# Experts' second layer in products of 512 columns, their outputs turned behind the loop, and POOL copying the gather's indices

## The reference

```python
h = (x_flat @ W_gat).reshape(M, HEADS, NUM_EXPERTS)
a_src = (h * att_src).sum(-1)
a_dst = (h * att_dst).sum(-1)
e = jax.nn.leaky_relu(a_src[src] + a_dst[dst], negative_slope=0.2)
e_max = jax.ops.segment_max(e, dst, num_segments=M)
ee = jnp.exp(e - e_max[dst])
denom = jax.ops.segment_sum(ee, dst, num_segments=M)
alpha = ee / (denom[dst] + 1e-16)
msg = h[src] * alpha[:, :, None]
agg = jax.ops.segment_sum(msg, dst, num_segments=M).reshape(M, HEADS * NUM_EXPERTS) + b_gat
scores = _layernorm(agg, ln_gamma, ln_beta).reshape(M, HEADS, NUM_EXPERTS).mean(1)
topk_s, topk_i = jax.lax.top_k(scores, TOP_K)
w = jax.nn.softmax(topk_s, axis=-1)
for ei in range(NUM_EXPERTS):
    g = jnp.where(topk_i == ei, w, 0.0).sum(-1)
    hh = jax.nn.gelu(x @ W1[ei] + b1[ei], approximate=False)
    out = out + g[..., None] * (hh @ W2[ei] + b2[ei])
```

## Time and profile before

| | |
|---|---|
| median of 3 runs | 1071.52 us (1070.34 to 1073.87) |
| the profiled execution: its own time | 1072.75 us |
| its span | 1071.0 us |
| busy in the span | PE 793.4 (74%), DVE 668.0 (62%), PEld 519.7 (49%), ACT 355.3 (33%), POOL 180.1 (17%) |
| granted TensorE clock, mean | 0.869 of full speed |

### The profile page before, as it was taken

How to read it: one execution, slowest core, us unless ns; L and a number is a source line. 1 busy time by engine, 2 the same in 40 slices (tenths; PEclk the granted TensorE clock), 3 DMA queues, 4 the chain that set the end, 5 groups by cost and what they waited for, 6 DMA issues and landing times.

```text
span 1071.0 us, 15105 instructions
## 1 busy us (share of the span) xinstructions
PE 793.4 (74%) x4837; PEld 519.7 (49%) x4837; DVE 668.0 (62%) x1393; ACT 355.3 (33%) x552; POOL 180.1 (17%) x179
## 2 busy tenths in 40 slices
PE   4369920017999989989988788799759877662688
PEld 1212220016887878878853233444327555442477
DVE  3599778755656656646648777595664434435764
ACT  3421130004544544545542333430022443333451
POOL 5180010000000000000022000100001366773021
PEclk9589965557999999999999899999977988886599
DMA  8000000001000000000000000000012200010001
GB/s 310 0 1 1 1 0 0 2 39 42 2 1 0 0 0 0 0 0 0 0 0 1 0 0 0 2 1 0 2 42 16 8 7 7 7 6 4 3 21 59
DMA packets 15645, 15.63 MB, mean 15 GB/s; under 512 B 9664, under 2 KB 13376, under 8 KB 15216
## 3 DMA queue, kind: packets, MB, share of 16 engines
q1 hardware_dynamic: 12544, 14.00, 4.3%
q0 software_dynamic: 3056, 1.08, 1.7%
HBM read 10.42 MB, written 4.65 MB: 14 GB/s over the span
## 4 chain that ended last, share of the span: by engine, by line
PE 19%; DVE 16%; issue 12%; POOL 3%; DMA 2%; DVEq 2%; ACT 2%; POOLq 0%; PEldq 0%; PEld 0%; SPq 0%; ACTq 0%
PE banks L1557 17%; DVE kept L1229 2%; POOL rows_g L592 2%; DMA rows_g<-table_d,g_idx 2%; DVE wide_buf L1189 1%; DVE wide_buf L1195 1%; PE banks L1838 1%; DVE tie L1193 1%; DVE kept L1292 1%; DVE kept L1386 1%; DVE T L867 1%; DVE round_k L1291 1%; PE banks L1590 1%; DVE shared L1384 1%; ACT wide_buf L776 1%
## 5 line engine op out<-in xcount | busy, mean ns | idle before, releaser
L1138 DVE TENSOR_TENSOR wide_buf<-banks,small 128x1024 f32<-128x1024 f32 x72 | 88.2, 1225 | 117.9 <-ACT small L726 117.9
L1557 PE MATMUL banks<-wide_buf 128*128 128x256 f32 (+1 forms) x720 | 144.6, 349 | 0.0
L1557 PEld LDWEIGHTS banks<-wide_buf 128*128 128x128 f32 x720 | 122.3, 194 | 12.6
L1557 PEld LDWEIGHTS banks<-XP 128*128 128x128 bf16 (+1 forms) x1552 | 101.8, 132 | 47.2 <-DVE XP L992 27.6
L1557 PE MATMUL banks<-XP 128*128 128x32 bf16 (+1 forms) x1552 | 102.4, 213 | 29.5 <-DVE XP L992 27.4
L592 POOL DMA_INDIRECT rows_g<-table_d,g_idx x88 | 95.5, 1085 | 132.2 <-issue 100.4
L1557 PE MATMUL banks<-taps_w,small 128*128 128x128 f32 x618 | 92.2, 296 | 21.0 <-issue 21.0
L1557 PE MATMUL banks<-T,XP 128*128 (+1 forms) x128 | 73.7, 701 | 38.2 <-ACT XP L789 33.3
L1557 PEld LDWEIGHTS banks<-taps_w,small 128*128 128x128 f32 x618 | 85.6, 203 | 31.7 <-issue 22.0
L724 ACT ACTIVATE small<-banks,neg_x 128x512 f32<-128x512 f32 x72 | 49.6, 690 | 150.1 <-PE banks L1557 124.2
L1557 PE MATMUL banks<-shared,sel 128*128 x216 | 60.2, 385 | 32.8 <-DVEq L1131 26.0
(11 more groups left out here) (330 smaller groups left out, 1190.9 us busy)
## 6 DMA issues: line engine op xcount, KB each, us to landing
wide_buf<-in_edges SPq DMA_DIRECT2D x2, 1536.0 KB, 15.4
generic_d<-generic SPq DMA_DIRECT2D x1, 2064.0 KB, 7.3
X<-in_x SPq DMA_DIRECT2D x4, 512.0 KB, 5.3
out_x<-X SPq DMA_DIRECT2D x4, 512.0 KB, 2.6
rows_g<-table_d,g_idx POOLq DMA_INDIRECT x88
wide_buf<-in_edges SPq DMA_DIRECT2D x2, 512.0 KB, 10.0
XP<-in_m_w SPq DMA_DIRECT2D x2, 512.0 KB, 4.7
taps_w<-in_w_dcn SPq DMA_DIRECT2D x1, 576.0 KB, 16.3
```

Source lines behind the costliest of these rows:

```text
L1138: nc.vector.tensor_tensor(near_w[s % RING], banks[:, 0:2, :], hat_x[:, h:h + 1, :].to_broadcast([P, 2, CHUNK]), ALU.mult).then_inc(w_done, 1)
L1557: return nc.tensor.matmul(o, l, r, start=start, stop=stop, **kw)
```

## The change

- `expert_out` swaps its operands: the second layer's weights stand, 512 columns of hidden values move, two products an expert. The output then has features in the partitions.
- All eight chunks of experts run in the loop before `slot_sums` (chunk 0 written out). Behind the loop `turn_outputs` transposes each of the 32 outputs in four blocks on PE, and ACT (`keep_turned`) copies them back to where they were. Nothing of the experts is left behind `slot_sums`, on PE or ACT.
- `bucket_dst` comes from 16 small products on PE between the second and third expert of chunk 0, and one copy on DVE, instead of two DMAs over memory. The numbering of slot partitions changes with it: `neg_lo` is now an input, one more small DMA of POOL at the start instead of an iota.
- In `slot_sums` partition `p` now goes to quarter `p // 32`: 32 successive products go to one quarter.
- POOL copies the indices from `slot_idx` to `g_idx` itself, four columns before each half's gathers, behind the wait for the buffer, and waits for its own copy. DVE copies none any more.
- A step on DVE picks the destination logits by half and ahead of the wait for that half's rows. `bucket_dst` is laid out so that the grid's inner dimension is contiguous.
- `slot_ends` moves ahead of the own attention terms, behind the new wait for the products (`dst_turned`).
- Outputs: for the fourth tile ACT scales the first expert's output, DVE adds the other three with three operations, and PE adds the result with one product instead of four.

```diff
-        bucket_dst = sb("bucket_dst", [P, HIS, HEADS])
+        bucket_dst = sb("bucket_dst", [P, HEADS, HIS])
...
-            sp.wait_ge(adst_ready, 1)
-            sp.dma_start(table_d_dst.rearrange("(t p) h -> p t h", p=P), a_dst[:, :, :]).then_inc(adst_in, 16)
             sp.wait_ge(table_out, 16)
             sp.dma_start(last_row[:, :], table_d[LAST].partition_broadcast(P)).then_inc(last_in, 16)
-            sp.wait_ge(adst_in, 16)
-            sp.dma_start(bucket_dst[:, :, :], table_d_dst.rearrange("(p t) h -> p t h", t=HIS)).then_inc(adst_in, 16)
...
-            def gather(asked, free):
+            def gather(g, r):
                 for half in range(2):
-                    pool.wait_ge(idx1_ready, asked + half + 1)
+                    cols = slice(half * HALF_STEP, (half + 1) * HALF_STEP)
+                    pool.wait_ge(max1_done, g * 2 + half + 1)
                     pool.sem_inc(passed, 1)
-                    pool.wait_ge(max1_done, free + half + 1)
+                    nc.gpsimd.tensor_copy(g_idx[:, cols], slot_idx[:, bass.ds(r * STEP + half * HALF_STEP, HALF_STEP)]).then_inc(idx1_ready, 1)
+                    pool.wait_ge(idx1_ready, g * 2 + half + 1)
                     pool.sem_inc(passed, 1)
...
-            with act.Fori(0, CHUNKS - 1) as i:
+            with act.Fori(0, CHUNKS) as i:
...
+            def keep_turned(first, last):
+                with act.Fori(first, last) as i:
+                    for e in range(EXPERTS):
+                        act.wait_ge(my_ready, 2 + CHUNKS * EXPERTS + EXPERTS * i + e + 1)
+                        nc.scalar.copy(y_exp[e][:, i, :], ps[2 + e][:, :]).then_inc(my_done, 1)
+            keep_turned(0, CHUNKS)
...
-                for e in range(EXPERTS):
-                    last = nc.scalar.activation(gate_diag[i % 2][:, 3, e, :], ident[:, :], ACT.Copy, scale=gate[:, 4 * i + 3, e:e + 1])
-                last.then_inc(diag_act, 1)
+                nc.scalar.activation(gate_diag[i % 2][:, 3, 0, :], y_exp[0][:, i, 3 * P:4 * P], ACT.Copy,
+                                     scale=gate[:, 4 * i + 3, 0:1]).then_inc(diag_act, 1)
...
+                for half in range(2):
+                    cols = bass.ds(r * STEP + half * HALF_STEP, HALF_STEP)
+                    grid = [P, HALF_STEP, HEADS, HIS]
+                    step(nc.vector.tensor_tensor(oh_slots, his[:, cols].unsqueeze(2).to_broadcast([P, HALF_STEP, HIS]),
+                                                 lane[:, 0:HIS].unsqueeze(1).to_broadcast([P, HALF_STEP, HIS]), ALU.is_equal))
+                    step(nc.vector.tensor_tensor(pick_grid, oh_slots.unsqueeze(2).to_broadcast(grid),
+                                                 bucket_dst[:, :, :].unsqueeze(1).to_broadcast(grid), ALU.mult))
+                    step(nc.vector.tensor_reduce(z_by_head[:, :, cols].rearrange("p h k -> p k h"), pick_grid, AX_X, ALU.add))
                     for landed in rows_landed[half]:
                         dve.wait_ge(landed, g * (16 * 2) + 16 * 2)
                         dve.sem_inc(passed, 1)
...
+            dve.wait_ge(dst_turned, 1)
+            run(nc.vector.tensor_copy(bucket_dst[:, :, :].rearrange("p h t -> p (h t)"), ps[6][:, 0:P]))
+            slot_ends()
...
+                dve.wait_ge(diag_act, i + 1)
+                last_tile = gate_diag[i % 2][:, 3, 0, :]
+                for e in range(1, EXPERTS):
+                    step = nc.vector.scalar_tensor_tensor(last_tile, y_exp[e][:, i, 3 * P:4 * P], gate[:, 4 * i + 3, e:e + 1], last_tile,
+                                                          ALU.mult, ALU.add)
...
-                for j in range(CHUNK // P):
-                    for c in range(2):
-                        last = mm(ps[4 + e % 2][:, j * P:(j + 1) * P], mid[:, e % 2, c, j * P:(j + 1) * P], m_w2[:, e, c, :], c == 0, c == 1)
+                for c in range(2):
+                    last = mm(ps[4 + e % 2][:, :], m_w2[:, e, c, :], mid[:, e % 2, c, :], c == 0, c == 1)
...
+            pe.wait_ge(adst_ready, 1)
+            for q in range(4):
+                part = slice(q * HIS, (q + 1) * HIS)
+                for h in range(HEADS):
+                    last = mm(ps[6][part, h * HIS:(h + 1) * HIS], a_dst[:, :, h], ident[:, part], True, True)
+            last.then_inc(dst_turned, 1)
...
+            def turn_outputs():
+                pe.wait_ge(my_done, 2 + CHUNKS * EXPERTS)
+                for i in range(CHUNKS):
+                    for e in range(EXPERTS):
+                        pe.wait_ge(my_done, 2 + CHUNKS * EXPERTS + EXPERTS * i + e - EXPERTS + 1)
+                        for j in range(CHUNK // P):
+                            last = nc.tensor.transpose(ps[2 + e][:, j * P:(j + 1) * P], y_exp[e][:, i, j * P:(j + 1) * P], ident[:, :])
+                        last.then_inc(my_ready, 1)
+            turn_outputs()
...
                 for p in range(P):
-                    j, q = divmod(p, 4)
+                    q, j = divmod(p, HIS)
                     c = j % (HIS // 2) * SUMS
                     last = mm(ps[j // (HIS // 2)][HIS * q:HIS * (q + 1), c:c + SUMS], oh_ends[:, p, :], sums_t[:, p, :], True, True)
...
-            experts(CHUNKS - 1)
...
+                for j in range(3):
                     for e in range(EXPERTS):
...
+                pe.wait_ge(diag_dve, 2 * i + 2)
+                mm(out_[:, 3 * P:4 * P], gate_diag[i % 2][:, 3, 0, :], ident[:, :], False, False, skip_group_check=True).then_inc(gated, 1)
```

82 lines of the change are left out of this document (31 added, 51 removed).

## The result

The changed kernel took 1081.01 us in the median of 8 runs (1076.07 to 1083.82), the kernel before 1071.72 (1068.65 to 1074.53): a ratio of 1.0076, 95% interval 1.0053 to 1.0099, **slower by 0.8%**. The profiled execution took 1081.13 us, its span is 1079.4. The forecast was 1060 us, range 1050 to 1088.

The account below looks back on a forecast made before the run. The prediction took POOL's indirect gathers to pace the stretch from 850.29 to 980.87 us. Its terms, -15.1 + 7 - 3.6 = -11.7 us, gave 1061.1 us profiled and 1060 us in the runs, range 1050 to 1088.

Parts of the forecast that it names:

- Part 3: Experts and turning, now all ahead of the scans: 15.0 us a chunk, hidden by some 4 us, so 0.
- The chosen case: The forecast itself, for the whole kernel: 1060 us, own range 1055 to 1067, chance 0.50.
- rival B: PE's signals held during gathers make experts plus turning the bound: 1098 us, or 1079 at a share of 0.8; chance 0.28.
- Part 1: Start of the gathers: POOL's second step begins at 841.5 us instead of 850.29.
- Part 2: Step of eight gathers: 12.3 us instead of 12.91; rows end at 965.8 instead of 980.87, -15.1 us with Part 1.
- rival C: Gather step doesn't shrink, copy and restart collide with DVE: 13.8 us a step, 1064 to 1074 us; chance 0.11.
- Part 4: Sum products on PE, 32 in a row to one quarter: slower by 7 us, at worst 11.3.
- Rival D: Sum products on PE: their order costs nothing, 1053 us in all; chance 0.11.
- Part 5: Tail: output chunks 4.0 us apart instead of 4.43, and less waiting for an exponential; -3.6 us together.

Follow-up runs that it names:

- A4: Changed kernel with the old experts' form (eight products of 128 columns, no turning) and the sums in A1's order: 1092.63 us; unchanged on another chip 1044.13 us.
- B4: Changed kernel with the second layer in eight products of 128 columns, weights still stationary, so four times as many PE instructions: 1129.60 us, ratio 1.0482.
- A1: Changed kernel with the 256 sum products issued in the old order, alternating over PE's quarters: 1072.68 us, ratio 0.9985.
- D: Changed kernel, C1, A3 and A4 run again unchanged on one chip: 1047.29, 1048.81, 1050.99 and 1044.13 us; kernel before 1070.17 us.
- E: Changed kernel and C1, with one other variant, run again unchanged on a fifth chip: 1050.07 and 1047.44 us; kernel before 1069.95 us.
- B2: Changed kernel with the 88 indirect DMAs replaced by plain DMAs of the same size from POOL, reading the table's start: 1042.86 us.
- B3: Changed kernel with the rows brought by plain DMAs that SyncE issues, reading the table's start: 1049.08 us.
- B1: Changed kernel with one more wait, so that POOL starts the gathers only after the experts' loop: 1164.73 us, longer by design.
- A3: Changed kernel with A1's order of sums and the turning moved behind the sums: 1063.43 us, ratio 0.9938; unchanged on another chip 1050.99 us.
- C1: A3 with the keeping of turned outputs split around the square root and the gates' exponential: 1048.81 us, ratio 0.9798.

## Why the prediction was right and wrong

**The step that failed is Part 3, "hidden, by some 4 us": 0.** It priced the loop at 15.0 a chunk and had it end at 942.4. Held, it ended at 976.1, 33.7 us later (seven chunks 138.6 instead of 105), ACT was free at 992.7 instead of 962.5, and with the cover gone each us counted, as the step itself had warned. Its undisturbed sizes were right: a chunk 15.05 us, all eight through at 938.1 to 945.4 wherever no chunk was held; the turning took 15.8, less than the 20 assumed. What was wrong is that the step took undisturbed prices although the rows of before showed chunks of 24.0 instead of 15.2. The chosen case needed the hold to go away; no row said that it would. 1081 us lies in the stated range only because the range had been drawn wide enough for rival B.

**Rival B named mechanism, place and mark** (ACT's keeping ends after the last row, DVE waits for an exponential). Its share, over five chunks beside gathers as in the rows of before, is 75.3 / 108.5 = 0.69 here (852.5 to 961.0 us), between its two values, 0.64 and 0.8, and the measured 1081 lies between their prices, 1098 and 1079. At 0.69 its formula gives about 1092; it had the turning 4 us too long and let the gathers hold from the start, where the chunk at 837.5 took 15.05 us. So the mechanism was right and its number close in part by luck. It had a chance of 0.28. Against it stood that POOL would pause twice as often and that signals, not passes, were late. Neither helped: the pauses were there and the hold with them, and two pauses of 0.99 us a step are less than the 2.9 us without a gather in a step of before. A4 shows chunks of 39 and 58 us for the old form beside the new gathers, B4 that the number of PE's instructions counts; that the new form's fewer ones kept the share above the 0.63 to 0.64 of before is argued from these two, not shown on one chip.

**Part 1**: POOL's second step, 15.7 us behind the first gather in the forecast, came 17.5 (held) and 16.7 (free) behind it, for 24.5 before: 1 to 2 us of the 8.8 are missing, in the held trace 1.45 of them by the late signal for the turned destinations.

**Part 2**: 11.5 us a step instead of 12.3. The sum had a slip: four gathers less the last pause, 4.7 us, with the copy's 0.15 and the restart's 0.85 make 5.7 us for half a step, not 5.9, and 5.7 is what an undisturbed half takes. Its upper bound of 13.8, and rival C's price with it, doesn't follow from its terms either (two halves of 5.7 and 1.4 are 14.2). Copy 0.20, restart 0.79, and hardly a collision: DVE's products are cut to 512 elements (0.69 us), and the longest gather took 1.39 us. Rival C falls. The rule of the Trainium skill (SBUF — State Buffer, "SBUF: two separate sides") that the two engines exclude each other would let a copy wait for at most one such product. The traces don't contradict it: the longest copy took 0.66 us, the mean one 0.24 held and 0.20 free beside 0.19 undisturbed, so the wait costs at most 0.05 us a copy. From second step to the exponents' operand it is 122.5 us held and 120.3 free against 134.0, so -11.5 and -13.7, where -6.3 was forecast; both parts together -18.5 held and -21.4 free, for -15.1.

**Part 4**: +5.3 and +5.5 for +7. The mechanism is shown by A1 and D (14.6 ns a pass in turns, 40 in a row); the 51 ns at the low clock and 30 at the full one lie near the two paces assumed, 59 and 29.4. The trace agrees with the rule of the Trainium skill (TensorEngine Tiling (Array Packing), "Key Properties") that different tiles work in parallel; giving it up costs 25 ns a pass in the mean. Rival D falls.

**Part 5**: -5.7 for -3.6. Output chunks are 3.76 apart, not 4.0: PE's passes follow each other without a gap, and the last chunk, for which DVE prepares nothing, takes 3.76 too. So PE sets the pace after all, though DVE's chain fills the same 3.76 us and has no slack left.

**The sum where nothing is held** is -21.4 + 5.5 - 5.6 = -21.5 for -11.7: the case that I took for the likeliest, nothing held, is what two chips show. But the 1047 and 1050 us measured there lie below that case's own range, 1055 to 1067, and at or below the lower end of the whole: Part 2 was too cautious by 7.4 us, Part 5 by 2, Part 4 by 1.5, and Part 1 too bold by 1. Nor is the turning hidden by 4 us there, only by the 1.4 that ACT waits: the rows come sooner too.

**What stays open.** What makes one chip hold and another not. On chips A, B and that of the first profile every kernel with indirect gathers beside PE's work was held, on C, D and E none, and the groups were run in that order, so chip and hour can't be told apart. The kernel before gives no hint: its timed runs are 1069.9 to 1071.7 everywhere, since its hold was covered.

One thing divides the traces exactly as the hold does. In every trace without held chunks, B2's and B3's on chip B among them, all 1,408 increments of the rows' landing are recorded; in the held ones, the kernel before's among them, it is 327 to 527. So the recording itself is another one where chunks are held. They are missing without PE's work too: in B1 PE is through at 998 us, and still only 0.22 of the increments that the gathers make are recorded from 1015 to 1030 us, as from 950 to 1011; from 1030 on it is 0.59. Whether the recording makes the signals late, or one cause makes them late and loses the records, is not shown. The Trainium skill (NOTIFIC — the notification-queue block, § 7.1) says that the pipeline inside the block which writes the records holds its producers rather than lose a record there. Late signals that grow with the number of instructions (B4) would fit that; records that are missing as well are not what it describes, and that plain DMAs from the same queue end the hold (B2) is not explained by it. Every timed run here carries a span and a granted clock, as a profiled one does, so none shows an unrecorded execution, and whether the hold exists in one was not tried.

Of the versions, A3 was faster than before where chunks are held (1063.4 against 1069.9) and is 4 us behind the changed kernel where they aren't; C1 equals the changed kernel where they aren't (1048.8 and 1047.4 against 1047.3 and 1050.1) and has A3's loop. C1 is the one that I would take; A4 is the fastest free (1044.1) and the slowest of these held (1092.6). What C1 does where chunks are held was not measured.

## What to carry to other kernels

Price a stage that you push under a cover at the pace that it shows under that cover, not at the pace of its quiet neighbours; if the two differ by more than the slack, the difference is the forecast. A "remote" releaser alone says that a record is missing; it is a late signal when PE's passes ended long before the wait did. Where that shows beside indirect gathers, give PE few, large instructions and put short dependent pieces (here the turning) where no gather runs; where nothing is held, the old form (A4 on chip D) was no slower. And run the unchanged kernel beside each variant on each chip: across chips, an edit worth 2 us (C1 over A3 on chip D) looked like 15.

## What the runs showed of the hardware

Beside indirect DMAs issued by POOL ACT waited up to 12.4 us at a time for a signal of PE (A4, B4), in the case shown 11.7 us past the end of the passes; beside plain DMAs of the same size from POOL (88 of them at 0.54 us each instead of 0.97) never over 1.1. In the traces with the long waits 63 to 77% of the rows' landing records are missing (356 of 1,408 are there in the first), in the others none. The hold grows with PE's instructions, compared across chips: seven chunks took 145 us with 32 matrix passes a chunk and 194 with 80, 112 unheld (table loads 816.2 to 961.0, 817.4 to 1011.4, 811.0 to 923.1). It is there on some chips, or at some hours, and absent on others, for the same file. The granted clock, 0.93 of 2.4 GHz from 843 to 960 us held and 0.99 free, is too near the full level in both for 30 us; held, PE and ACT are both busy for less of the time (windows as in the earlier trace rows, held, then free; the free one has turned outputs in it).

```profile
843.00:960.00 117.00, 88.24 (x185) 35.32 (x183) 40.81 (x102) 49.68 (x72) 82.82 (x99) 0.93 0.12 7
```

```profile
843.00:960.00 117.00, 104.05 (x334) 51.48 (x332) 42.63 (x103) 75.01 (x118) 76.61 (x94) 0.99 0.11 7
```
